# A dynamic 3x3 convolution on 16 images: a larger descriptor scratch for accumulating DMAs, packed small columns, and a new hand-written order of work

## The chip, the cores and the metric

The kernel runs on one core of one Trainium2 chip. The time is the device time of one launch in microseconds (us). Of the kernel before there are three timed runs and one profiled execution.

## What is computed

`x` is (16, 256, 56, 56) float32, the weights are (4, 256, 256, 3, 3) float32: four sets, mixed anew for each image.

```python
def _L0_conv_ref(x, weight, att_w, att_b):
    pooled = jnp.mean(x, axis=(2, 3))
    att = jax.nn.sigmoid(pooled @ att_w.T + att_b)
    agg_w = jnp.einsum('nk,kocij->nocij', att, weight)
    ...                      # one 3x3 convolution per image, stride 1, padding 1
...
def _gn(v, G=32, eps=1e-5):  # per image and group of 8 channels
    ...
    return ((g - m) / jnp.sqrt(s + eps)).reshape(v.shape)
...
x = x + _L0_conv_ref(_gn(x), L0_conv_weight, L0_conv_att_w, L0_conv_att_b)
```

## The kernel before

**Tiling.** The 256 channels are two halves (`c` on the input side, `o` on the output side) of 128 partitions. An image is two chunks of 28 rows. A chunk is convolved along its rows with a transform of six points (`NC` = 6, tables `ORDER`, `POINT`): six transformed inputs `Vs` and six transformed weights `Us`, each split in a high and a low float16 part. For each chunk, point and output half, TensorE runs one `group(e, k, o)` of 18 matmuls of 392 columns (L390); `k` is 0 to 5 for chunk 0 and 6 to 11 for chunk 1, so one step has 24 groups. Six products of high and low parts (3 products by 2 input halves) by three column shifts make up the 18.

**Steps.** `epoch(e)` on each engine convolves image e-1 (in buffer `b`) and prepares image e (in buffer 1-b). There are 16 of them, 14 in a loop that holds two. To prepare an image, VectorE takes the channel statistics (`stats`, L549, eight calls of two instructions; `channel_stats`, L557 writes `mv`), TensorE averages `mv` over the groups (`group_mean_mm`, L342), VectorE and ScalarE turn that into scale and shift (`group_shift`, `group_variance`, `norm_scale`, `attention`), ScalarE normalizes `X` in place (`norm`, L848), TensorE mixes the four weight sets (`mix`, L365, three units) and ScalarE takes the result to `G` (`take_taps`, L842).

**Transformed operands.** VectorE builds an item in one of four buffers `E` (`v_single`, `v_pair` from `X`; `u_pair` from `G`), ScalarE rounds it to float16 (`v_high` L803, `u_high` L809, L813), and VectorE writes the rest (`v_low` L540, `u_low` L534). Points 0 and 5 of the weights need no item.

**Results.** A finished group lies in one of four PSUM banks. ScalarE (`take_first`, `take_pair`) and VectorE (`take_other` L598, `take_edge` L617, `add_rows` L605) combine the groups, and the output rows overwrite `X[b]`. When all rows of one chunk and half stand there, GpSimd issues a DMA that adds the original `x` from DRAM to them (`add_input`, L974, `accum_op`). When this has landed, SyncE stores the rows (L310), and when the store has landed it loads the same place with the image after the next (L303). SyncE goes through this in order: for each chunk store half 0, store half 1, load half 0, load half 1. `add_input` of chunk 1 waits for `("rows", 9, o)`, `("edge", 10, o)` and `("edge", 11, o)`.

**What sets the order.** All order is written out by hand: the tables `E_ITEMS`, `V_LO`, `U_LO`, `V_HI`, `U_HI`, `ACT_TAKES`, `DVE_TAKES` and the bodies of `epoch` on each engine. Each engine works its list strictly in turn, and waits are on counts computed from the tables. On VectorE the statistics of chunk 1 of the next image stand after `take_other(e, 2, 0)`; they are the first instructions that need the loads of the end of the step before.

Of the kernel before, what the change touches and what calls it, by code (L numbers as in the profile page):

```python
# [10 lines left out]
M = 4  # L11
# [67 lines left out]
    (0, 0, 0), (0, 0, 5), (0, 1, 1), (0, 1, 2), (0, 1, 5), (0, 1, 3), (0, 1, 4), (0, 1, 0),  # L79
# [3 lines left out]
    (0, 0, 0), (0, 1, 0), (0, 1, 4), (0, 1, 5), (1, 0, 1), (1, 0, 2), (1, 0, 3), (1, 0, 4),  # L83
    (1, 1, 1), (1, 1, 2), (1, 0, 5), (1, 1, 3),
# [3 lines left out]
    (0, 0), (0, 1), (2, 0), (1, 0), (1, 1), (2, 1), (3, 0), (3, 1),  # L88
    (6, 1), (6, 0), (7, 0), (8, 0), (7, 1), (8, 1), (9, 0), (9, 1),
# [33 lines left out]
def conv_kernel(nc, x, w, att_w, att_b, out):  # L123
# [3 lines left out]
    with ExitStack() as ctx:  # L127
# [19 lines left out]
        attb = sb("attb", [P, 1], F32)  # L147
        nattb = sb("nattb", [P, 1], F32)
        wmax = sb("wmax", [P, CT * JT], F32)
        wtop = sb("wtop", [P, 1], F32)  # L150
        wall = sb("wall", [P, 1], F32)
        ws = sb("ws", [P, 4], F32)
        us = sb("us", [P, 8], F32)
        bn = sb("bn", [P, CT, 8, 6], F32)
        seen = sb("seen", [P, 1], F32)
        mv = sb("mv", [P, CT, 2], F32)
        nmean = sb("nmean", [P, CT], F32)
        rstd = sb("rstd", [P, CT], F32)
        shift = sb("shift", [P, CT], F32)
        off = sb("off", [P, CT], F32)  # L160
        sq = sb("sq", [P, CT], F32)
        spread = sb("spread", [P, CT], F32)
        var = sb("var", [P, CT], F32)
        std0 = sb("std0", [P, CT], F32)
        rs0 = sb("rs0", [P, CT], F32)
        quo = sb("quo", [P, CT], F32)
        std = sb("std", [P, CT], F32)
        rs1 = sb("rs1", [P, CT], F32)
        pooled = sb("pooled", [P, CT], F32)
        ex = sb("ex", [P, 1], F32)  # L170
        ex1 = sb("ex1", [P, 1], F32)
        att = sb("att", [P, 1], F32)
# [9 lines left out]
                   + [X[1][:, i, 1:HP - 1, :].rearrange("p r w -> p (r w)")[:, 0:WG] for i in range(2)])  # L182
# [45 lines left out]
        def rows(b, chunk, i):  # L228
            r = CR * chunk + i
            return [X[b][:, c, r:r + M * (TR - 1) + 1:M, :] for c in range(CT)]  # L230

        def out_rows(b, chunk, o, r):
            q = CR * chunk + 1 + r
            return X[b][:, o, q:q + M * (TR - 1) + 1:M, :]

        def held(b, chunk, c):
            return X[b][:, c, 1 + CR * chunk:1 + CR * (chunk + 1), :].rearrange("p r w -> p (r w)")
# [101 lines left out]
        def _(pe):  # L339
# [56 lines left out]
            def epoch(e, more):  # L396
# [23 lines left out]
                group(e, 7, 1)  # L420
                if more:
                    mix(e, 1)
                group(e, 8, 0)
# [34 lines left out]
        def _(dve):  # L458
# [84 lines left out]
            def stats(e, b, chunk, c, part):  # L543
# [3 lines left out]
                for q in (2 * part, 2 * part + 1):  # L547
                    r = 1 + CR * chunk + TR * q
                    ins = dve.bn_stats(bn[:, c, 4 * chunk + q, :],  # L549
                                       X[b][:, c, r:r + TR, :].rearrange("p r w -> p (r w)"))  # L550
# [70 lines left out]
            def epoch(e, b, more):  # L621
                steps[0] = 0
                v_single(e, b, ("V", 0, 0, 0))
                v_low(e, (0, 0, 4))
                if more:
                    stats(e, 1 - b, 0, 0, 0)
                u_low(e, (0, 0, 0))
                if more:
                    stats(e, 1 - b, 0, 0, 1)
                v_single(e, b, ("V", 0, 0, 5))  # L630
                v_low(e, (0, 0, 0))
                u_low(e, (0, 1, 0))
                if more:
                    stats(e, 1 - b, 0, 1, 1)
                u_low(e, (0, 1, 4))
                v_pair(e, b, ("V", 0, 1, 1))
                take_other(e, 2, 0)
                if more:
                    stats(e, 1 - b, 1, 0, 0)
                    stats(e, 1 - b, 1, 1, 0)  # L640
                    stats(e, 1 - b, 1, 0, 1)
                    stats(e, 1 - b, 0, 1, 0)
                    stats(e, 1 - b, 1, 1, 1)
                take_other(e, 3, 0)
                if more:
                    channel_stats(e)
# [378 lines left out]
```

## Time and profile before

| | |
|---|---|
| median of 3 runs | 1504.98 us (1502.47 to 1506.42) |
| profiled execution | 1503.41 us, of which the span of the trace is 1501.8 us |
| TensorE busy | 89% of the span |
| VectorE busy | 86% |
| ScalarE busy | 45% |
| GpSimd busy | 4% |
| mean granted TensorE clock | 0.959 of full speed |

In the traces PE is TensorE (PEld its weight loads), DVE is VectorE, ACT is ScalarE, POOL is GpSimd, SP is SyncE. A name such as "X<-x_dram" is output and input of an instruction. The number in brackets behind a row of the timeline is the idle time of the engine before it and what ended it; "issue" there means that the engine waited for nothing that the profile shows.

### The profile page before, as it was taken

The page shows a single profiled execution, that of the slowest core. Times are in us where ns is not written, and L with a number is a line of the kernel's source. Part 1 is how long each engine was busy: PE and PEld are TensorE (multiplying, and loading weights), DVE is VectorE, ACT ScalarE, POOL GpSimd, SP SyncE. Part 2 cuts the span into 40 slices and gives each one's busy share as a digit, 9 for nine tenths or more (in the row PEclk, how much of TensorE's full clock was granted, in tenths as well). Part 3 has the DMA queues.
Part 4 walks back from the last instruction along what each step waited for, and adds up shares of the span by engine and source line. Part 5 has one row for each costly group of instructions (what it writes and reads, how often), then busy time and mean ns, then how long its engine had stood idle before and what let it go on. Part 6 is the DMA issues. An engine that isn't in the chain of part 4 may idle for free. (4 is left out here: it accounts for less than half of the span.)

```text
span 1501.8 us, 24616 instructions
## 1 busy us (share of the span) xinstructions
PE 1330.2 (89%) x8808; PEld 743.0 (49%) x8808; DVE 1296.6 (86%) x2211; ACT 669.7 (45%) x922; POOL 59.1 (4%) x77
## 2 busy tenths in 40 slices
PE   0479989899898989989898998989899898998995
PEld 0145545455454545545454554555455454554553
DVE  7999979798997979889798997979899797989961
ACT  2645445363443536344263534426354452634430
POOL 0000000000000000000000000000000000000000
PEclk9989999999999999999999999999999999999998
DMA  8202514445152443515344351544525144451425
GB/s 341 85 2 50 144 65 130 130 121 138 30 149 82 130 129 87 156 36 138 103 129 131 65 140 55 143 116 129 129 50 145 67 129 129 112 146 36 100 61 150
DMA packets 29349, 165.50 MB, mean 110 GB/s; under 512 B 3360, under 2 KB 3616, under 8 KB 28192
## 3 DMA queue, kind: packets, MB, share of 16 engines
q0 software_dynamic: 9216, 51.38, 20.3%
q1 hardware_dynamic: 20000, 112.34, 20.2%
q8 instruction: 84, 1.38, 0.4%
q14 instruction: 49, 0.40, 0.1%
HBM read 112.33 MB, written 51.38 MB: 109 GB/s over the span
## 5 line engine op out<-in xcount | busy, mean ns | idle before, releaser
L390 PE MATMUL pM<-Vs,Us 128*128 128x392 f16 x6912 | 1212.0, 337 | 21.6 <-DVE Us L534 12.8
L390 PEld LDWEIGHTS pM<-Vs,Us 128*128 128x128 f16 x6912 | 678.4, 99 | 543.1 <-issue 60.7
L803 ACT CAST Vs<-E 128x784 f16<-128x784 f32 x192 | 161.8, 843 | 214.7 <-DVE E L509 146.5
L549 DVE BATCH_NORM_STATS2 bn<-X 128x6 f32<-128x392 f32 x256 | 127.2, 555 | 90.2 <-DMA X<-x_dram 90.2
L540 DVE TENSOR_TENSOR Vs<-E,Vs 128x784 f16<-128x784 f32 x192 | 186.4, 971 | 19.3 <-ACT Vs L803 19.3
L483 DVE SCALAR_TENSOR_TENSOR T<-X 128x392 f32<-128x392 f32 x384 | 193.8, 560 | 2.4 <-issue 1.6
L831 ACT ACTIVATE X<-pM,us 128x392 f32<-128x392 f32 x128 | 75.2, 587 | 211.6 <-PE pM L390 211.6
L365 PE MATMUL pG<-W,D 128*32 128x512 f16 x1728 | 103.8, 385 | 30.9 <-DVE W L762 30.9
L813 ACT CAST Us<-E 128x768 f16<-128x768 f32 x128 | 104.5, 828 | 51.1 <-PE pM L390 35.3
L509 DVE SCALAR_TENSOR_TENSOR E<-T 128x784 f32<-128x784 f32 x128 | 119.1, 972 | 3.5
L534 DVE SCALAR_TENSOR_TENSOR Us<-E,Us 128x768 f16<-128x768 f32 x128 | 120.1, 949 | 0.2
L524 DVE SCALAR_TENSOR_TENSOR E<-G,T 128x768 f32<-128x768 f32 x128 | 117.0, 955 | 3.4
L974 POOL DMA_DIRECT2D X<-x_dram x64 | 56.5, 883 | 1393.2 <-DVE X L605 775.3
L848 ACT ACTIVATE X<-X,shift,rstd 128x1568 f32<-128x1568 f32 x64 | 106.4, 1689 | 0.0
L842 ACT ACTIVATE G<-pG 128x512 f32<-128x512 f32 x144 | 80.4, 594 | 25.5 <-PE pG L365 25.2
L342 PE MATMUL pS<-mv,avg 128*128 128x2 f32 x32 | 9.1, 353 | 93.2 <-DVE mv L557 78.3
L365 PEld LDWEIGHTS pG<-W,D 128*32 128x32 f16 x1728 | 42.2, 97 | 84.1 <-DVE W L762 31.4
L852 ACT ACTIVATE std<-var 128x2 f32<-128x2 f32 x16 | 3.3, 203 | 177.2 <-DVE var L569 177.2
L483 DVE SCALAR_TENSOR_TENSOR E<-X,T 128x392 f32<-128x392 f32 x128 | 66.8, 564 | 5.4
L518 DVE SCALAR_TENSOR_TENSOR T<-G 128x768 f32<-128x768 f32 x64 | 60.8, 951 | 0.2
L534 DVE SCALAR_TENSOR_TENSOR Us<-G,Us 128x768 f16<-128x768 f32 x64 | 60.6, 949 | 0.0
L809 ACT ACTIVATE Us<-G 128x768 f16<-128x768 f32 x64 | 53.6, 837 | 14.0 <-PE pM L390 14.0
(65 smaller groups left out, 518.0 us busy)
## 6 DMA issues: line engine op xcount, KB each, us to landing
X<-x_dram SPq DMA_DIRECT2D x64, 784.0 KB, 5.5
X<-x_dram POOLq DMA_DIRECT2D x64, 784.0 KB, 7.8
out_dram<-X SPq DMA_DIRECT2D x64, 784.0 KB, 3.4
W<-w_dram SPq DMA_DIRECT2D x6, 1152.0 KB, 18.2
X<-w_dram SPq DMA_DIRECT2D x2, 1152.0 KB, 26.1
attw<-attw_dram SPq DMA_DIRECT2D x1, 128.0 KB, 8.5
attb<-attb_dram SPq DMA_DIRECT2D x1, 0.5 KB, 10.1
```

What stands on the lines that cost most here:

```text
L365: mm = pe.matmul(dst, D[:, a, :], mix_part(W16[:, :, j, b * WG:(b + 1) * WG], m), start=(a == 0 and b == 0), stop=(a == 1), tile_position= ...
L390: mm = pe.matmul(tile_rows(bank(k, o)), Us[:, j, a, c, o, kx, :], v_in(j, b, c, kx), start=(at < 2 and n == 0), stop=(n == 3 * KS * CT - 1 ...
L483: ins = dve.scalar_tensor_tensor(out=dst[c], in0=a[c], scalar=scale, in1=d[c], op0=ALU.mult, op1=ALU.add)
L509: dve.scalar_tensor_tensor(out=dst, in0=T2[:, :], scalar=POINT[j + m], in1=T1[:, :], op0=ALU.mult, op1=ALU.add).then_inc(e_ready, 1)
L524: dve.scalar_tensor_tensor(out=dst, in0=G[:, c, :, 1, :], scalar=scale, in1=halves(t), op0=ALU.mult, op1=last).then_inc(e_ready, 1)
L534: dve.scalar_tensor_tensor(out=u_flat(j, 1, c), in0=src, scalar=scale, in1=u_flat(j, 0, c), op0=ALU.mult, op1=ALU.subtract).then_inc(u_lo, 1)
L540: dve.tensor_tensor(v_out(v[2], 1), e_planes(("V", *v)), v_out(v[2], 0), ALU.subtract).then_inc(v_lo, 1)
L549: ins = dve.bn_stats(bn[:, c, 4 * chunk + q, :], X[b][:, c, r:r + TR, :].rearrange("p r w -> p (r w)"))
L803: act.copy(v_out(j, 0), e_planes(("V", *v))).then_inc(v_hi, 1)
L813: act.copy(u_flat(j, 0, c), halves(e_buf(("U", *u)))).then_inc(u_hi, 1)
L842: act.mul(mix_part(G[:, :, :, :, :].rearrange("p c o k n -> p c (o k n)"), m), src, MIX_SCALE).then_inc(taps_taken, 1)
L848: act.activation(y, y, ACT.Identity, bias=shift[:, c:c + 1], scale=rstd[:, c:c + 1]).then_inc(normed, 1)
```

## The change

Five things are changed.

1. `dynamic_dma_scratch_size` is 1024 bytes for 512. It is the memory in which GpSimd writes the descriptors of its DMAs.
2. `X` is one tensor: neighbouring halves share one row of zeros, and one strided memset replaces four.
3. Nineteen small tensors are columns of one tensor `small`.
4. On TensorE, `mix(e, 1)` stands between the two halves of k = 7 (it stood behind both), and `mix(e, 2)` behind `group(e, 10, 0)` (it stood behind k = 8).
5. The tables and the lists of VectorE and ScalarE are written in another order. The set of instructions of a step is the same. One item, `("V", 1, 0, 0)`, is now built at the end of a step for the next one, and ScalarE rounds seven weight items at the beginning of the next step that it rounded at the end of the step.

```diff
 DVE_TAKES = [
-    ("other", 2, 0), ("other", 3, 0), ("other", 2, 1), ("other", 3, 1), ("edge", 4, 0),
-    ("edge", 4, 1), ("edge", 5, 0), ("rows", 3, 1), ("edge", 5, 1), ("rows", 3, 0),
-    ("other", 8, 0), ("other", 8, 1), ("other", 9, 0), ("other", 9, 1), ("rows", 9, 0),
-    ("edge", 10, 0), ("edge", 10, 1), ("rows", 9, 1), ("edge", 11, 0), ("edge", 11, 1),
+    ("other", 2, 0), ("other", 2, 1), ("other", 3, 0), ("other", 3, 1), ("edge", 4, 0),
+    ("edge", 4, 1), ("edge", 5, 0), ("rows", 3, 1), ("rows", 3, 0), ("edge", 5, 1),
+    ("other", 8, 0), ("other", 8, 1), ("other", 9, 0), ("other", 9, 1), ("edge", 10, 0),
+    ("rows", 9, 1), ("edge", 10, 1), ("edge", 11, 0), ("edge", 11, 1), ("rows", 9, 0),
 ]
...
-        X = [sb(f"X{b}", [P, CT, HP, W], F32) for b in range(2)]
+        Xs = sb("X", [P, 2 * CT * (HP - 1) + 1, W], F32)
...
-        us = sb("us", [P, 8], F32)
+        small = sb("small", [P, 72], F32)
...
+        us = small[:, 16:24]
...
                 group(e, 7, 0)
+                if more:
+                    mix(e, 1)
                 group(e, 7, 1)
-                if more:
-                    mix(e, 1)
                 group(e, 8, 0)
                 group(e, 8, 1)
-                if more:
-                    mix(e, 2)
                 group(e, 9, 0)
                 group(e, 9, 1)
                 group(e, 10, 0)
+                if more:
+                    mix(e, 2)
                 group(e, 10, 1)
...
-            for b in range(2):
-                dve.memset(X[b][:, :, 0:1, :], 0.0)
-                dve.memset(X[b][:, :, HP - 1:HP, :], 0.0)
+            dve.memset(Xs[:, 0:2 * CT * (HP - 1) + 1:HP - 1, :], 0.0)
...
-    nc = bacc.Bacc("TRN2", target_bir_lowering=False, num_devices=1, dynamic_dma_scratch_size=512)
+    nc = bacc.Bacc("TRN2", target_bir_lowering=False, num_devices=1, dynamic_dma_scratch_size=1024)
```

**VectorE from the last edges of a step on.** First before, the end of the second step in the loop (L605 is `add_rows`, L617 with TA is `take_edge` of k = 11, half 0 and then half 1, L540 is `v_low`, L534 is `u_low`):

```order
L605 SCALAR_TENSOR_TENSOR X<-TB,X 128x7x56 [waits dve_took]
L605 SCALAR_TENSOR_TENSOR X<-TA,X 128x7x56
L612 REGISTER_ALU
L616 REGISTER_ALU [waits dve_took]
L617 SCALAR_TENSOR_TENSOR X<-pM,us,TA 128x7x56 [waits group_done]
L539 REGISTER_ALU
L540 TENSOR_TENSOR Vs<-E,Vs 128x2x7x56 [waits v_hi]
L616 REGISTER_ALU [waits dve_took]
L617 SCALAR_TENSOR_TENSOR X<-pM,us,TA 128x7x56 [waits group_done]
L534 SCALAR_TENSOR_TENSOR Us<-E,Us 128x768 [waits u_hi]
```

and of the changed kernel, from `take_edge` of k = 11, half 1 (L619) to `add_rows` of k = 9, half 0 (L607); L520 and L526 are `u_pair`, L536 is `u_low`:

```order
L619 SCALAR_TENSOR_TENSOR X<-pM,small,TA 128x7x56 [waits group_done]
L481 REGISTER_ALU [waits taps_taken]
L520 SCALAR_TENSOR_TENSOR T<-G 128x768 [waits e_ready]
L466 REGISTER_ALU
L526 SCALAR_TENSOR_TENSOR E<-G,T 128x768 [waits u_lo,dve_step]
L526 SCALAR_TENSOR_TENSOR E<-G,T 128x768 [waits u_lo]
L531 REGISTER_ALU
L536 SCALAR_TENSOR_TENSOR Us<-E,Us 128x768 [waits u_hi]
L531 REGISTER_ALU
L536 SCALAR_TENSOR_TENSOR Us<-E,Us 128x768 [waits u_hi]
L607 SCALAR_TENSOR_TENSOR X<-TB,X 128x7x56 [waits dve_took]
L607 SCALAR_TENSOR_TENSOR X<-TA,X 128x7x56
```

`add_rows(e, b, 9, 0)` stood ahead of all four last edges; it now stands behind the last of them, with one `u_pair` and two `u_low` between.

**VectorE at the statistics that need the last loads.** Before (L598 is `take_other`, L549 `stats`; x_in10 and x_in11 count the loads of chunk 1, halves 0 and 1):

```order
L598 SCALAR_TENSOR_TENSOR TA<-pM,us,TA 128x392 [waits act_took]
L549 BN_STATS bn<-X 128x6 [waits x_in10,mean_ready]
L549 BN_STATS bn<-X 128x6
L549 BN_STATS bn<-X 128x6 [waits x_in11,mean_ready]
...
L549 BN_STATS bn<-X 128x6 [waits x_in01,mean_ready]
...
L598 SCALAR_TENSOR_TENSOR TB<-pM,us,TB 128x392 [waits act_took]
...
L555 COPY seen<-bn 128x1 [waits pieces_ready]
L557 BN_AGGR mv<-bn 128x2 x2
```

and of the changed kernel (L551 `stats`, L600 `take_other`, L536 `u_low` of point 0, L559 the end of `channel_stats`):

```order
L551 BN_STATS bn<-X 128x6 [waits x_in11,mean_ready]
L551 BN_STATS bn<-X 128x6
L599 REGISTER_ALU
L600 SCALAR_TENSOR_TENSOR TA<-pM,small,TA 128x392 [waits act_took]
...
L531 REGISTER_ALU
L536 SCALAR_TENSOR_TENSOR Us<-G,Us 128x768 [waits u_hi]
L551 BN_STATS bn<-X 128x6 [waits x_in10,mean_ready]
...
L600 SCALAR_TENSOR_TENSOR TA<-pM,small,TA 128x392 [waits act_took]
...
L559 BN_AGGR mv<-bn 128x2 x2
```

The statistics of half 1, whose load is the last one, are now the first that need chunk 1, and they stand ahead of the `take_other(e, 2, 0)` that group (4, 0) waits for and of the `u_low(e, (0, 0, 0))` that it needs as weights.

## Rows read from the trace of the kernel before

**Rows 1.** Waits over the whole run: who waited for whom, total us, times, longest.
```profile
POOL X L974 <- issue: 195.6, 31, 6.7
DVE bn L549 <- DMA X<-x_dram: 90.2, 30, 6.2
PE pS L342 <- DVE mv L557: 78.3, 14, 6.9
```

**Rows 2.** Timeline of TensorE, one step: start us, us, instructions [idle before].
```profile
599.78 12.64 PE L390 MATMUL pM<-Vs,Us 128*128 128x392 f16 x74
613.45 27.50 PE L390 MATMUL pM<-Vs,Us 128*128 128x392 f16 x162 [1.03 <-issue]
645.73 0.58 PE L342 MATMUL pS<-mv,avg 128*128 128x2 f32 x2 [4.79 <-DVE mv L557]
646.21 5.35 PE L390 MATMUL pM<-Vs,Us 128*128 128x392 f16 x18
...
664.13 2.12 PE L365 MATMUL pG<-W,D 128*32 128x512 f16 x36
```

**Rows 3.** Timeline of GpSimd over the loop: starts of the accumulating DMAs.
```profile
172.35 0.87 POOL L974 DMA_DIRECT2D X<-x_dram  x1 [26.25 <-DVE X L617]
...
1326.77 0.89 POOL L974 DMA_DIRECT2D X<-x_dram  x1 [26.63 <-DVE X L617]
```

**Rows 4.** The same view, the pair of chunk 1 at the step of rows 2.
```profile
616.13 0.89 POOL L974 DMA_DIRECT2D X<-x_dram  x1 [26.50 <-DVE X L617]
623.57 0.88 POOL L974 DMA_DIRECT2D X<-x_dram  x1 [6.56 <-issue]
```

**Rows 5.** Timeline of SyncE's DMA queue, the stores and loads behind that pair.
```profile
623.41 9.24 SPq L310 DMA_DIRECT2D out_dram<-X  x2
632.84 3.83 SPq L303 DMA_DIRECT2D X<-x_dram  x2
```

**Rows 6.** Timeline of VectorE, same step: last edges and the two waits for loads.
```profile
615.30 0.97 DVE L540 TENSOR_TENSOR Vs<-E,Vs 128x784 f16<-128x784 f32 x1
616.18 0.62 DVE L617 SCALAR_TENSOR_TENSOR X<-pM,us,TA 128x392 f32<-128x392 f32 x1
616.72 0.95 DVE L534 SCALAR_TENSOR_TENSOR Us<-E,Us 128x768 f16<-128x768 f32 x1
...
638.30 1.04 DVE L549 BATCH_NORM_STATS2 bn<-X 128x6 f32<-128x392 f32 x2 [4.54 <-DMA X<-x_dram]
640.74 3.84 DVE L549 BATCH_NORM_STATS2 bn<-X 128x6 f32<-128x392 f32 x8 [1.41 <-DMA X<-x_dram]
```

**Rows 7.** Windows: busy us and instructions of each engine, granted clock, DMA share, GB/s.
```profile
617.50:623.00 5.50, 5.50 (x34) 3.22 (x33) 5.15 (x10) 2.73 (x4) 0.00 (x0) 1.00 0.87 150
624.00:626.00 2.00, 2.00 (x14) 1.14 (x13) 1.88 (x5) 0.00 (x0) 0.45 (x1) 1.00 0.90 364
626.00:631.50 5.50, 5.50 (x34) 3.16 (x33) 5.46 (x10) 2.28 (x4) 0.00 (x0) 1.00 0.93 160
632.00:642.00 10.00, 8.94 (x54) 4.98 (x51) 4.05 (x8) 5.13 (x7) 0.00 (x0) 1.00 0.69 241
```

**Rows 8.** Timeline of VectorE: starts from which the lengths of its items are read.
```profile
683.69 0.95 DVE L518 SCALAR_TENSOR_TENSOR T<-G 128x768 f32<-128x768 f32 x1
...
686.42 0.62 DVE L598 SCALAR_TENSOR_TENSOR TA<-pM,us,TA 128x392 f32<-128x392 f32 x1
...
695.72 1.99 DVE L483 SCALAR_TENSOR_TENSOR T<-X 128x392 f32<-128x392 f32 x4
...
699.52 0.62 DVE L617 SCALAR_TENSOR_TENSOR X<-pM,us,TB 128x392 f32<-128x392 f32 x1
```

**Rows 9.** Windows around the wait of TensorE; the columns are those of rows 7.
```profile
643.90:650.70 6.80, 4.97 (x16) 2.57 (x17) 5.96 (x15) 0.00 (x0) 0.00 (x0) 0.50 0.01 2
```

**Rows 10.** Timelines of TensorE where the loop begins, and of GpSimd at the end.
```profile
84.97 5.41 PE L390 MATMUL pM<-Vs,Us 128*128 128x392 f16 x16 [12.83 <-DVE Us L534]
...
1482.57 0.88 POOL L974 DMA_DIRECT2D X<-x_dram  x1 [17.08 <-DVE X L617]
```

More of the change, by code:

```diff
@@ L622, in epoch @@
                 steps[0] = 0
-                v_single(e, b, ("V", 0, 0, 0))
-                v_low(e, (0, 0, 4))
+                v_single(e, b, ("V", 0, 0, 5))
+                u_low(e, (0, 1, 4))
                 if more:
                     stats(e, 1 - b, 0, 0, 0)
-                u_low(e, (0, 0, 0))
-                if more:
-                    stats(e, 1 - b, 0, 0, 1)
-                v_single(e, b, ("V", 0, 0, 5))
+                    stats(e, 1 - b, 0, 1, 1)
+                v_pair(e, b, ("V", 0, 1, 1))
                 v_low(e, (0, 0, 0))
@@ L676, in epoch @@
                 v_low(e, (0, 1, 4))
+                v_low(e, (0, 1, 0))
                 if more:
@@ L679, in epoch @@
                     v_low(e, (1, 0, 1))
-                    u_low(e, (1, 0, 1))
                 take_other(e, 8, 0)
                 if more:
+                    u_low(e, (1, 0, 1))
+                    u_low(e, (1, 0, 2))
                     v_low(e, (1, 0, 2))
-                    u_low(e, (1, 0, 2))
+                    v_pair(e, 1 - b, ("V", 1, 0, 3))
                     u_pair(e, ("U", 1, 0, 3))
+                    v_low(e, (1, 0, 4))
                 take_other(e, 8, 1)
                 if more:
-                    u_low(e, (1, 0, 3))
+                    v_low(e, (1, 0, 3))
+                take_other(e, 9, 0)
+                take_other(e, 9, 1)
+                take_edge(e, b, 10, 0)
+                add_rows(e, b, 9, 1)
+                if more:
                     u_pair(e, ("U", 1, 1, 1))
-                take_other(e, 9, 0)
-                if more:
                     u_low(e, (1, 0, 4))
-                take_other(e, 9, 1)
-                add_rows(e, b, 9, 0)
-                take_edge(e, b, 10, 0)
-                if more:
-                    u_low(e, (1, 1, 2))
-                    u_low(e, (1, 1, 1))
-                    v_pair(e, 1 - b, ("V", 1, 0, 3))
                 take_edge(e, b, 10, 1)
                 if more:
-                    u_pair(e, ("U", 1, 1, 3))
-                add_rows(e, b, 9, 1)
+                    u_low(e, (1, 1, 1))
                 take_edge(e, b, 11, 0)
                 if more:
-                    v_low(e, (1, 0, 3))
+                    u_low(e, (1, 0, 3))
                 take_edge(e, b, 11, 1)
                 if more:
+                    u_pair(e, ("U", 1, 1, 3))
+                    u_low(e, (1, 1, 2))
                     u_low(e, (1, 1, 3))
+                add_rows(e, b, 9, 0)
+                if more:
+                    v_single(e, 1 - b, ("V", 1, 0, 0))
                 assert steps[0] == STEPS or not more, steps
@@ L769, in _ @@
             u_low(0, (1, 0, 1))
+            u_low(0, (1, 0, 2))
             v_low(0, (1, 0, 2))
-            u_low(0, (1, 0, 2))
+            v_pair(0, 0, ("V", 1, 0, 3))
             u_pair(0, ("U", 1, 0, 3))
-            u_low(0, (1, 0, 3))
+            v_low(0, (1, 0, 4))
+            v_low(0, (1, 0, 3))
             u_pair(0, ("U", 1, 1, 1))
             u_low(0, (1, 0, 4))
+            u_low(0, (1, 1, 1))
+            u_low(0, (1, 0, 3))
+            u_pair(0, ("U", 1, 1, 3))
             u_low(0, (1, 1, 2))
-            u_low(0, (1, 1, 1))
-            v_pair(0, 0, ("V", 1, 0, 3))
-            u_pair(0, ("U", 1, 1, 3))
-            v_low(0, (1, 0, 3))
             u_low(0, (1, 1, 3))
+            v_single(0, 0, ("V", 1, 0, 0))
             first[0] = steps[0]
@@ L881, in epoch @@
                 if more:
-                    norm(e, 1 - b, 1, 0)
-                v_high(e, (0, 1, 4))
-                if more:
-                    norm(e, 1 - b, 0, 1)
+                    norm(e, 1 - b, 1, 1)
                     norm(e, 1 - b, 0, 0)
@@ L888, in epoch @@
                 if more:
-                    norm(e, 1 - b, 1, 1)
+                    norm(e, 1 - b, 1, 0)
                     take_taps(e, 0)
-                take_first(e, 6, 1)
-                if more:
                     take_taps(e, 1)
                     take_taps(e, 2)
+                    norm(e, 1 - b, 0, 1)
                 take_first(e, 6, 0)
@@ L897, in epoch @@
                     take_taps(e, 3)
+                v_high(e, (0, 1, 4))
+                take_first(e, 7, 1)
                 take_first(e, 7, 0)
```

178 lines of the change are left out of this document (86 added, 92 removed), and 8 rows, old and new, of the table E_ITEMS.

## The prediction

> **What bounds the kernel now.** I read the waits first, then the timelines of one step, then the windows. The steps are regular: from the first accumulating DMA of chunk 1 at 172.35 to the same at 1326.77 are 13 steps, 88.80 us each [rows 3]. TensorE has no room apart from one hole. In the step shown it ends the step before at 599.78 + 12.64 = 612.42, runs nine groups (162 matmuls in 27.50 us, 3.06 us a group), then stands for 4.79 us until `mv` is there [rows 2]. The engine's granted clock is at half, its lower level of 1.2 GHz, from about 643.9 to 650.7 [rows 9]: the next group takes 5.35 us instead of 3.1, so the hole costs about 2.1 us more. Without both the step would be some 81 us. `mv` is late because VectorE waits for loads: 90.2 us in all, two waits a step, here 4.54 and 1.41 us [rows 1, 6]. VectorE itself has little room too. Its waits in this step are 5.95 for loads and some 3.2 others, so it works 79.6 us of 88.8. So the last loads set the step, through VectorE, and both engines are close behind.
>
> The loads hang on a chain that I call C, from the first accumulating DMA of chunk 1 to the statistics that need the last load: 616.13 to 640.74, 24.6 us [rows 4, 6]. In it GpSimd starts the second accumulation only at 623.57, after 6.56 us "for nothing that the profile shows" [rows 4]; there are 31 such waits, 195.6 us [rows 1]. That wait ends just after the first store starts at 623.41 [rows 5], which needs the first accumulation landed: the second waits until the first is done. The larger scratch is meant for this.
>
> **Part 1, the scratch.** If it works, the second issue moves from 623.57 to about 617.0, 6.5 us earlier. The gain in C is less, since the DMA engines are not idle meanwhile. The first accumulation holds all 16 for 5.5 x 0.87 = 4.8 us, the store of half 0 for 2.0 x 0.90 = 1.8, the second accumulation for 5.5 x 0.93 = 5.1, the rest (one store, two loads) for 10 x 0.69 = 6.9 [rows 7]. That is 18.6 us of work, with 1.4 before the first packet (616.13 to 617.5): C can hardly be under 20.0, or 19.6 if the start of the second, for which the engines need some time, hides behind the first transfer. In the worst case it has no such cover and shares the engines with the first store: the gain is then only the gap between the transfers and what the engines leave idle, about 2 us, and C = 22.6. I take 21.0, near the sum of work plus one latency of 1.0 us that stays between landing and the next issue (the first transfer leaves the engines at about 622.5, the store starts at 623.41 [rows 5, 7]). So the gain is 3.6 us of the 6.5.
>
> The Trainium skill says the same of any two transfers at once ("DMA: Bandwidth & Descriptors", section "Rules for kernel authors"): two transfers to disjoint parts serialize, because both spread over the same 16 engines. Taken strictly it speaks against the purpose of this change; the 0.87 and 0.93 of rows 7 agree with it. By the rule alone C would be at its upper end.
>
> **Part 2, VectorE's order ahead of C.** This is a loss. Lengths, from start to start [rows 6, 8]: `u_pair` 686.42 - 683.69 = 2.73, `v_pair` 699.52 - 695.72 = 3.80, `v_low` 0.88, `u_low` 0.87 (0.01 less, as it is 2% shorter), edge 616.72 - 616.18 = 0.54. One `stats` is a quarter of 3.84 less its overlap, 0.94 [rows 6]. The others go by kind: `add_rows` is two instructions of 392 columns, 0.95; `take_other` reads 392 columns of PSUM as the edge does, 0.53; `v_single` is four instructions of 392 columns and one wait between, 1.99 and 0.16 [rows 8], 2.15. Call P the end of the last group of a step. Before, the edge of half 0 stood at 615.30 less 0.54, and C began at P + 3.7 (612.42 to 616.13). Now the first add_input also waits for `add_rows(9, 0)`, which stands last: edge 0.1 + 0.54, `u_pair` 2.73, two `u_low` 1.74, two rows 1.03, GpSimd 0.2. C begins at P + 6.3, if VectorE has caught up with TensorE. That is 2.6 us later.
>
> **Part 3, VectorE's order behind C.** Between the start of C and the first statistics that need the last load VectorE has, less the 0.2: two `v_single` 4.3, two `u_low` 1.74, four `stats` 3.8, `v_pair` 3.8, `v_low` 0.88, together 14.5 us. C is 21.0, so VectorE waits about 6.5 us (before: 5.95). Worse, the half asked for first is now the later one, and `take_other(2, 0)` and `u_low(0, 0, 0)`, for which group (4, 0) waits, stand behind that wait. Call t the landing of the last load. `stats` 0.94, `take_other` 0.53, `stats` 0.94, `u_low` 0.87 and the latency give group (4, 0) at t + 3.4. Then come 3.1 for the group and 0.5 for the mean; `mv` is ready at t + 6.3 and no longer in the way. TensorE is at group (4, 1) at t + 7.0 plus the slow clock. Before, it was there at 646.21 - 640.74 = t + 5.5 [rows 2, 6]. The rest of the step, from group (4, 1) at 646.21 to the next P at 612.42 + 88.8 = 701.2, is 55.0 us, with about 2 us of slow clock in it, which now falls mostly on group (4, 0). So the next P is at t + 62.0 on TensorE. On VectorE: 79.6 of work less 20.6 between the last edge and t is 59.0, and I find waits of 0.3 and 1.3 for the two group averages, 1.0 for the last `norm`, which now stands behind three `take_taps`, and 0.5 for an item rounded late: t + 62.1. Both ends meet; I take 62.0.
>
> **The step.** 6.3 + 21.0 + 62.0 = 89.3 us, 0.5 more than 88.8. From P to P there are 14 such intervals: 7.0 us.
>
> **Part 4, the rest.** The mixes are moved on TensorE alone: 2.06 us each, 36 matmuls as before [rows 2], with nothing new late behind them: `take_first` and `take_taps` come 1 us or more ahead of need, `u_pair(1, 1, 1)`, which now needs the third unit, stands 2 us behind it. Cover gone, each us costs 14. The loop starts at 84.97 on TensorE, released by a `u_low` of VectorE [rows 10]. Ahead of that one, VectorE now has a `v_pair` and two `v_low` more and two `u_low` fewer: 3.8 + 1.76 - 1.74 = 3.8, of which I count 3.5, as the first groups run on a slow clock (16 matmuls in 5.41). At the end, C's head is cut by 3.6 but begins about 4 us later relative to the last group, since `add_input` waits for rows behind the last edge and the first accumulation no longer runs beside the last group (1482.57 [rows 10]): +0.5. The shared zero row takes three short memsets away, at a place where VectorE then waits for the loads of x: nothing. The packed columns change no instruction: nothing, between -0.1 and +0.1.
>
> **Sum.** 1501.8 + 7.0 + 3.5 + 0.5 = 1512.8 of span, and 1.6 outside it as before (1503.41 less 1501.8): **1514.4 us**. The profiled execution is 1.6 below the median of the runs, so this may be read as 1516 against 1504.98; I stay with the trace.
>
> **Rivals.**
> *The transfers truly overlap* (this one ends faster). If the second accumulation ends about a store's time or less after the first, C falls below 20.2, where the longer start is paid back. At C = 19.6: step 87.9, 1514.4 - 14 x 1.4 = 1494.8 us. If it landed 1 us behind the first, C = 17.1 and 1460 us. For it: in the engines' work the accumulation moves only 150 to 160 GB/s, the store 364 [rows 7], so the engines spend their time on something that two transfers might share. Against it: they are busy 0.87 and 0.93. Chance 0.22.
> *The steps lock in at no change.* C between 20.2 and 20.7, or a shorter stay at the low clock: the low stretch is 6.8 us wide and TensorE stands in part of it [rows 9]. If TensorE stands 6 us instead of 4.8, less of it hits work; up to 1 us a step. 1501 to 1509 us. Chance 0.17.
> *The scratch does not do it* (the wait comes from something else). C stays 24.6, while the order is made for less: step 92.9, 14 x 3.6 = 50 more, 1565 us. For it: the row only says "issue". Against it: the wait ends with the landing each time. Chance 0.05.
> *The two accumulations stay strictly one behind the other and behind the first store*, as the rule above has it. C is 22.6, the step 90.9: 1514.4 + 14 x 1.6 = 1536.8 us. For it: 0.87 and 0.93 busy. Against it: 1.4 us of start-up that can hide. Chance 0.06.
> *VectorE falls behind in the second half.* It has some 0.7 us to spare where group (10, 1) waits for `take_other(8, 1)`, and 1.1 us where group (1, 0) waits for `u_low(1, 1, 3)` behind the last edge. Waits of ScalarE that I place wrongly come out there. 1 us a step more is 1528, 1.5 is 1535. Chance 0.14.
> The forecast itself, 1509 to 1524: 0.36.
>
> **How the numbers follow.** A measurement of this kernel can tell about 0.3%, 4.5 us, from no change: 1500.5 to 1509.5. Faster is the first rival, 0.22; same is the second, 0.17; slower are the forecast and the last three, 0.36 + 0.05 + 0.06 + 0.14 = 0.61. The range takes in C from 19.4 to 22.8 and leaves out 0.09 below (C under 19.4) and 0.09 above (no effect of the scratch, and a late VectorE beyond 1.8 us a step): 1492 to 1540.
>
> **What the profile would show.** GpSimd's "issue" waits of 6.3 us gone, the second accumulation 0.9 to 1.0 us behind the first (part 1). The first of chunk 1 at P + 6.3 (part 2). C from 19.6 to 22.6, and about 14 waits for loads of 6 to 7 us at the statistics of half 1, with almost none behind (part 3). TensorE's hole ahead of group (4, 0), about 6 us, put down to VectorE's `Us` or `take_other`, and none at the mean. The loop starting near 88.5. I am wrong if C comes out under 20, if TensorE stands anywhere in the second half of a step, or if the second issue still waits.

## The result and the profile after

The changed kernel takes 1509.41 us (median of 19 runs, 1505.4 to 1516.5), the kernel before in the same sessions 1505.19 us (19 runs). The ratio is 1.0032, with a 95% interval from 1.0019 to 1.0044: slower by 0.3%, 4 to 5 us. The span of the profiled execution is 1510.1 us, 8.3 more than before. The forecast was 1514.4 us.

A small difference, but not a small change. Waits over the whole run after, as in [rows 1]:

```profile
DVE bn L551 <- DMA X<-x_dram: 91.8, 16, 8.9
DVE T L485 <- issue: 13.0, 6, 2.4
PE pM L392 <- DVE Us L536: 113.2, 19, 15.5
```

The 195.6 us in which GpSimd waited for nothing that the profile shows are gone. The wait for the loads has stayed as it was, 91.8 us for 90.2, now nearly all in one wait a step. TensorE's hole has moved from the mean of the groups to group (4, 0), where it waits for `u_low(0, 0, 0)` (L536), and has grown from 78.3 us to 95 in the 14 steps (the 113.2 also hold the 15.5 ahead of the first step and some short waits).

Timeline of GpSimd after: the first pair of chunk 1, one in the middle, and the last but one (rows 3 and 4 show the same of before).

```profile
178.84 1.77 POOL L969 DMA_DIRECT2D X<-x_dram  x2 [36.20 <-DVE X L607]
...
892.62 1.77 POOL L969 DMA_DIRECT2D X<-x_dram  x2 [36.65 <-DVE X L607]
...
1426.77 1.76 POOL L969 DMA_DIRECT2D X<-x_dram  x2 [36.71 <-DVE X L607]
```

Both DMAs of a pair start in one piece of 1.77 us. From 178.84 to 1426.77 are 14 steps of 89.14 us in the mean. Before, the same 14 took 1414.97 - 172.35, 88.76 us each. The 14 steps after are not alike: eleven take 88.4 to 89.1 us, 88.76 in the mean and so as much as before, and three take 90.3 to 90.7. In two of these three the granted clock of TensorE is low for 10.2 us, from 643.6 and from 1357.0, where it is low for 6.8 in all others; in the third the chain C takes 22.6 us. The step shown below is one of the eleven (88.68 us).

Timeline of TensorE in the step of 892.62 (as [rows 2]):

```profile
883.78 26.14 PE L392 MATMUL pM<-Vs,Us 128*128 128x392 f16 x154
916.90 4.72 PE L392 MATMUL pM<-Vs,Us 128*128 128x392 f16 x18 [6.98 <-DVE Us L536]
921.46 0.28 PE L344 MATMUL pS<-mv,avg 128*128 128x2 f32 x2
921.60 3.20 PE L392 MATMUL pM<-Vs,Us 128*128 128x392 f16 x18
```

and of VectorE there (as [rows 6]):

```profile
885.90 0.62 DVE L619 SCALAR_TENSOR_TENSOR X<-pM,small,TA 128x392 f32<-128x392 f32 x1
886.44 0.95 DVE L520 SCALAR_TENSOR_TENSOR T<-G 128x768 f32<-128x768 f32 x1
...
891.38 0.56 DVE L607 SCALAR_TENSOR_TENSOR X<-TA,X 128x392 f32<-128x392 f32 x1
...
913.40 1.04 DVE L551 BATCH_NORM_STATS2 bn<-X 128x6 f32<-128x392 f32 x2 [7.11 <-DMA X<-x_dram]
914.36 0.61 DVE L600 SCALAR_TENSOR_TENSOR TA<-pM,small,TA 128x392 f32<-128x392 f32 x1
914.88 1.03 DVE L551 BATCH_NORM_STATS2 bn<-X 128x6 f32<-128x392 f32 x2
915.83 0.94 DVE L536 SCALAR_TENSOR_TENSOR Us<-G,Us 128x768 f16<-128x768 f32 x1
```

The last edge stands at 885.90, the rows that `add_input` waits for at 891.38, the chain C begins at 892.62 and ends at 913.40: 20.8 us. VectorE stands 7.11 us for the last load. Only behind it come `take_other` and the `u_low` at 915.83 that lets TensorE go on at 916.90. Its group then takes 4.72 us, since the clock is low; this is the window as in [rows 9]:

```profile
914.90:921.80 6.90, 4.90 (x22) 2.57 (x23) 6.90 (x15) 0.00 (x0) 0.00 (x0) 0.63 0.00 0
```

SyncE's queue behind the pair, as [rows 5], and the DMA engines in windows that begin about with the pair's packets, as [rows 7]; the second window overlaps the first a little:

```profile
899.77 4.12 SPq L312 DMA_DIRECT2D out_dram<-X  x2
905.47 3.77 SPq L305 DMA_DIRECT2D X<-x_dram  x2
```

```profile
894.00:903.00 9.00, 9.00 (x55) 5.18 (x53) 8.93 (x16) 1.81 (x3) 0.39 (x1) 1.00 1.01 201
902.30:908.00 5.70, 5.70 (x36) 3.32 (x34) 4.00 (x7) 4.04 (x7) 0.00 (x0) 1.00 0.98 348
908.00:914.20 6.20, 1.92 (x12) 0.88 (x9) 0.80 (x2) 2.84 (x4) 0.00 (x0) 0.92 0.59 202
```

The two stores start 7.15 us and 10.9 us behind the first accumulation (before: 7.3 and 16.2). Up to 908 the engines are busy 1.01 and 0.98 of the time, for 0.87 to 0.93 before: no gap is left between the accumulations and the first store. Behind that, to the landing of the last load, they are busy 0.59.

### The profile page after: what moved, and what is told of

Its sections match the earlier page's. It is cut to its first block, busy times and chain, and to the rows that moved or that the text cites. A ratio compares the mean times of both kernels' runs of the same rounds, so it can differ in the third digit from the quotient of the medians.

```text
span 1510.1 us, 24711 instructions
## 1 busy us (share of the span) xinstructions
PE 1322.8 (88%) x8808; PEld 738.8 (49%) x8808; DVE 1297.8 (86%) x2208; ACT 674.2 (45%) x922; POOL 59.6 (4%) x77
## 3 DMA queue, kind: packets, MB, share of 16 engines
q0 software_dynamic: 9216, 51.38, 18.2%
## 4 chain that ended last, share of the span: by engine, by line
PE 42%; DVE 24%; DMA 18%; issue 12%; ACT 1%; DVEq 1%; POOL 0%; POOLq 0%; SPq 0%; ACTq 0%
PE pM L392 38%; DMA X<-x_dram 14%; PE pG L367 4%; DVE Us L536 4%; DMA out_dram<-X 4%; DVE E L526 3%; DVE T L520 3%; DVE T L485 3%; DVE Vs L542 2%; DVE X L607 2%; DVE X L619 2%; DVE E L511 1%; DVE bn L551 1%; DVE TA L600 1%; DVE W L762 1%
## 5 line engine op out<-in xcount | busy, mean ns | idle before, releaser
L392 PE MATMUL pM<-Vs,Us 128*128 128x392 f16 x6912 | 1210.2, 337 | 115.6 <-DVE Us L536 113.2
L551 DVE BATCH_NORM_STATS2 bn<-X 128x6 f32<-128x392 f32 x256 | 127.0, 554 | 91.8 <-DMA X<-x_dram 91.8
L833 ACT ACTIVATE X<-pM,small 128x392 f32<-128x392 f32 x128 | 75.2, 588 | 172.6 <-PE pM L392 155.4
L536 DVE SCALAR_TENSOR_TENSOR Us<-E,Us 128x768 f16<-128x768 f32 x128 | 120.1, 950 | 2.9 <-ACT Us L815 1.5
L526 DVE SCALAR_TENSOR_TENSOR E<-G,T 128x768 f32<-128x768 f32 x128 | 116.9, 954 | 2.2
L850 ACT ACTIVATE X<-X,small 128x1568 f32<-128x1568 f32 x64 | 106.4, 1688 | 0.0
L854 ACT ACTIVATE small<-small 128x2 f32<-128x2 f32 x16 | 3.3, 206 | 186.8 <-DVE small L571 186.8
L520 DVE SCALAR_TENSOR_TENSOR T<-G 128x768 f32<-128x768 f32 x64 | 61.0, 952 | 7.6 <-ACT G L844 6.8
L825 ACT ACTIVATE TA<-pM,small 128x392 f32<-128x392 f32 x64 | 37.6, 588 | 52.7 <-PE pM L392 49.4
L536 DVE SCALAR_TENSOR_TENSOR Us<-G,Us 128x768 f16<-128x768 f32 x64 | 58.5, 933 | 2.2 <-ACT Us L811 2.2
```

The lines of the kernel that those rows point to most:

```text
L392: mm = pe.matmul(tile_rows(bank(k, o)), Us[:, j, a, c, o, kx, :], v_in(j, b, c, kx), start=(at < 2 and n == 0), stop=(n == 3 * KS * CT - 1 ...
L520: step(e, dve.scalar_tensor_tensor(out=halves(t), in0=G[:, c, :, 2, :], scalar=p * p, in1=G[:, c, :, 0, :], op0=ALU.mult, op1=ALU.add))
L526: dve.scalar_tensor_tensor(out=dst, in0=G[:, c, :, 1, :], scalar=scale, in1=halves(t), op0=ALU.mult, op1=last).then_inc(e_ready, 1)
L536: dve.scalar_tensor_tensor(out=u_flat(j, 1, c), in0=src, scalar=scale, in1=u_flat(j, 0, c), op0=ALU.mult, op1=ALU.subtract).then_inc(u_lo, 1)
L551: ins = dve.bn_stats(bn[:, c, 4 * chunk + q, :], X[b][c][:, r:r + TR, :].rearrange("p r w -> p (r w)"))
L850: act.activation(y, y, ACT.Identity, bias=shift[:, c:c + 1], scale=rstd[:, c:c + 1]).then_inc(normed, 1)
```

## The experiments

All times are medians; ratios are to the kernel before on the same chip. "The changed kernel" stands for 1509.4 us. The kernel before took 1505.1, 1505.8 and 1507.4 us on the three chips used, so a difference between two edited kernels can come out some 2 to 4 us otherwise by the medians than by the ratios.

**The scratch alone, in the order of before.** The kernel before with `dynamic_dma_scratch_size=1024`, `Xs` and `small`, none of the tables or lists changed.

```diff
-    nc = bacc.Bacc("TRN2", target_bir_lowering=False, num_devices=1, dynamic_dma_scratch_size=512)
+    nc = bacc.Bacc("TRN2", target_bir_lowering=False, num_devices=1, dynamic_dma_scratch_size=1024)
```

> The kernel before in its own order of work, with the scratch of 1024 bytes (and, to make room for it, the shared zero rows and the packed columns). Chain theory (the step is set by the chain C from the first accumulating DMA of chunk 1 to the statistics of the last load, and VectorE's work behind it): C falls from 24.6 to 21.0 us while it begins where it did, 3.7 us after the last group P. VectorE's waits for loads fall from 6.0 to about 2.4 us a step; the step is 21.0 + 64.2 = 85.2 us, 14 x 3.6 = 50 us less: 1452 us. Order theory (the new order is needed for the gain): it stays at 1500 to 1505 us. Clock theory (TensorE's low clock gives back what a shorter wait wins, steps stay at 88.7 us): 1500 to 1505 us.

Measured: 1443.83 us, ratio 0.959 (0.956 to 0.963). Its wait for the loads:

```profile
DVE bn L551 <- DMA X<-x_dram: 39.4, 29, 2.9
```

and the timeline of GpSimd, the pair of chunk 1 in one step:

```profile
682.61 0.88 POOL L974 DMA_DIRECT2D X<-x_dram  x1 [32.80 <-DVE X L619]
684.12 0.88 POOL L974 DMA_DIRECT2D X<-x_dram  x1 [0.63 <-issue]
```

So the scratch brings 61 us, and the new order costs 66. The waits for loads fall from 90.2 to 39.4 us as expected. C is 21.1 us in the mean of the 14 steps. The time is 8 us under the forecast of 1452, since 63.4 us are left behind C for the 64.2 that were expected. TensorE's hole is shorter, and the low clock with it: 3.4 us long in ten steps and absent in four, for 6.8 us in each before (mean granted clock 0.978 for 0.959). The order theory and the clock theory, both at 1500 or more, fall.

**The packing alone.** As before, with 512 bytes.

```diff
-        X = [sb(f"X{b}", [P, CT, HP, W], F32) for b in range(2)]
+        Xs = sb("X", [P, 2 * CT * (HP - 1) + 1, W], F32)
...
-        attb = sb("attb", [P, 1], F32)
+        small = sb("small", [P, 72], F32)
```

> The kernel before with the shared zero rows and the packed columns alone: scratch of 512 bytes, the order of before. By the prediction's part 4 this changes nothing: 1503 to 1507 us. The rival reading of before_scratch (that part of its gain comes from the packing and not from the scratch) wants under 1500 us.

Measured: 1509.14 us beside 1505.8, ratio 1.0012 (0.9992 to 1.0032): no difference that can be told. The interval would allow one as large as that of the whole change (1.0032); in the trace the 14 steps take 88.67 us each, no more than before, so there is none in the steps.

**The changed kernel with 512 bytes.**

```diff
-    nc = bacc.Bacc("TRN2", target_bir_lowering=False, num_devices=1, dynamic_dma_scratch_size=1024)
+    nc = bacc.Bacc("TRN2", target_bir_lowering=False, num_devices=1, dynamic_dma_scratch_size=512)
```

> The changed kernel with the scratch of 512 bytes again. Chain theory: GpSimd's waits of some 6.3 us for nothing that the profile shows return, C is 24.6 us for 21.0, the step 92.8 us, 14 x 3.6 = 50 us more than the changed kernel: 1560 us. Theory that two accumulations at once gain nothing since both use the same 16 DMA engines: 1510 us. Clock theory: 1510 to 1525 us.

Measured: 1575.22 us, ratio 1.045 (1.043 to 1.048). Its waits:

```profile
POOL X L969 <- issue: 209.9, 32, 7.7
DVE bn L551 <- DMA X<-x_dram: 151.0, 15, 12.4
```

The waits of GpSimd are back, 6.6 us each, and VectorE's wait for the loads is 10.6 us a step for 6.3. That is 66 us for the scratch in this order, 15 more than forecast. C is 25.1 us in the mean for the 24.6 of the forecast, and with a hole of 11 us instead of 7 TensorE spends longer at the low clock: 10.2 or 13.7 us a step for 6.8 (0.935 in the mean).

**`add_rows` of k = 9, half 0 ahead of the last edges again.**

```diff
-    ("other", 8, 0), ("other", 8, 1), ("other", 9, 0), ("other", 9, 1), ("edge", 10, 0),
-    ("rows", 9, 1), ("edge", 10, 1), ("edge", 11, 0), ("edge", 11, 1), ("rows", 9, 0),
+    ("other", 8, 0), ("other", 8, 1), ("other", 9, 0), ("other", 9, 1), ("rows", 9, 0), ("edge", 10, 0),
+    ("rows", 9, 1), ("edge", 10, 1), ("edge", 11, 0), ("edge", 11, 1),
...
+                add_rows(e, b, 9, 0)
                 take_edge(e, b, 10, 0)
...
                     u_low(e, (1, 1, 3))
-                add_rows(e, b, 9, 0)
```

> The changed kernel with add_rows of k = 9, half 0 ahead of the last four edges, where it stood before the change (and so in the table of takes). Chain theory: C begins at about P + 0.2 us for P + 7.0, its length stays 21 us, so the last load lands 6.8 us earlier; VectorE waits for it about 1 to 2 us for 6.1, group (4, 0) on TensorE comes almost without a hole, the step is bound by VectorE's 79.6 us of work and its other waits, 83 to 84.5 us: 1430 to 1450 us. Theory that the place of add_rows does not matter (C's end is set elsewhere): 1505 to 1512 us.

Measured: 1437.22 us, ratio 0.955 (0.953 to 0.957), in the range of the chain theory. Two instructions, 1 us together, moved in VectorE's list are worth 72 us. The steps are no longer alike, 81 to 83 and 85 to 88 us in turn. The timeline of VectorE where the loop begins anew shows why:

```profile
429.38 1.04 DVE L485 SCALAR_TENSOR_TENSOR T<-X 128x392 f32<-128x392 f32 x2
430.45 1.04 DVE L485 SCALAR_TENSOR_TENSOR E<-X,T 128x392 f32<-128x392 f32 x2
436.10 1.04 DVE L485 SCALAR_TENSOR_TENSOR T<-X 128x392 f32<-128x392 f32 x2 [4.61 <-issue]
```

VectorE stands 4.61 us ahead of the first instruction behind the loop's edge, six times in the run, at every second step; before it was 1.6 us in all six.

**The half that lands last asked for last.**

```diff
                     stats(e, 1 - b, 0, 0, 1)
-                    stats(e, 1 - b, 1, 1, 1)
                 take_other(e, 2, 0)
-                if more:
-                    stats(e, 1 - b, 1, 1, 0)
                 u_low(e, (0, 0, 0))
                 if more:
                     stats(e, 1 - b, 1, 0, 0)
                     stats(e, 1 - b, 1, 0, 1)
+                    stats(e, 1 - b, 1, 1, 1)
+                    stats(e, 1 - b, 1, 1, 0)
```

> The changed kernel with take_other(2, 0) and u_low(0, 0, 0) ahead of the statistics of chunk 1, and of these half 0 ahead of half 1. C is untouched. Chain theory: group (4, 0) starts without a wait, the hole of 7 us ahead of it is gone and one of some 3.5 us comes ahead of the mean of the groups; after the last load VectorE has 3.3 us less to do, so the step is 3.3 to 3.6 us shorter, 85.5 us: 1459 us. Theory that only the start and length of C count: 1505 to 1510 us.

Measured: 1464.72 us, ratio 0.974 (0.972 to 0.976). Its waits:

```profile
PE pS L344 <- DVE mv L559: 44.8, 14, 5.2
DVE bn L551 <- DMA X<-x_dram: 41.6, 26, 3.4
PE pM L392 <- DVE Us L536: 17.6, 5, 15.5
```

The hole is ahead of the mean again, 3.2 us a step for 7, and the one ahead of group (4, 0) is gone. The pairs of chunk 1 start at 179.19 and 1376.28 in this kernel's timeline, 14 steps of 85.5 us, which is the forecast. "Only start and length of C count" falls: who stands behind the wait counts too.

**Filling the hole.** 24 matmuls on old operands ahead of group (4, 0) in the changed kernel; then 36.

```diff
+                if more:
+                    keep_clock(24)
                 group(e, 4, 0)
```

> The changed kernel with 24 matmuls on old operands, 384 columns each (about 4 us), ahead of group (4, 0), so in the hole of about 7 us in which TensorE stands; nothing waits for them. Clock theory (the low clock behind the hole is what sets the step): group (4, 0) takes 3.1 us again for 4.8 to 6.0, the step is 1.7 to 2.9 us shorter: 1470 to 1487 us. Chain theory (VectorE sets the step; TensorE's slow group costs it only its wait of 0.9 us for the variance and the long low stretches of two steps): 1492 to 1503 us. If the clock does not care: 1509 us.

Measured: 1517.36 us, ratio 1.007 (1.005 to 1.010): a miss for every theory. The timeline of TensorE in one step:

```profile
736.77 2.11 PE L440 MATMUL pS<-W 128*128 128x384 f16 x12
742.74 4.83 PE L392 MATMUL pM<-Vs,Us 128*128 128x392 f16 x18 [3.86 <-DVE Us L538]
```

3.86 us of the hole are left, and group (4, 0) still takes 4.83 us. The clock is low for only 3.4 us in most steps, but from 742.7 here, so wholly on the group. The edit didn't keep the clock up where TensorE works, so it doesn't show what the low clock costs. Its own cost is in the trace: the first pair of chunk 1 starts 3.7 us later than in the changed kernel (182.53 for 178.84), as the fillers of the first step stand ahead of it, and the 14 steps take 89.39 us each for 89.14, which adds 3.5.

```diff
+                if more:
+                    keep_clock(36)
                 group(e, 4, 0)
```

> As filler with 36 matmuls (5.8 us) in the hole, so that about 1.2 us of it is left. With 24, group (4, 0) still took 4.8 us in most steps (a low stretch of 3.4 us that fell wholly on it), and in the one step where it took 3.2 us the step was 87.9 us instead of 89.3. If the clock can be kept up by this, group (4, 0) takes 3.1 to 3.2 us in most steps and these are 87.9 us: about 14 x 1.3 = 18 us less than the changed kernel, and some 6 more in the first step, where the fillers run slowly: 1495 to 1500 us. If VectorE alone sets the step: 1510 to 1516 us.

Measured: 1502.4 us, ratio 0.996 (0.994 to 0.998), so 7 us under the changed kernel by the medians and 11 by the ratios. The timeline and the window:

```profile
641.19 6.01 PE L440 MATMUL pS<-W 128*128 128x384 f16 x36
648.14 3.21 PE L392 MATMUL pM<-Vs,Us 128*128 128x392 f16 x18 [0.94 <-DVE Us L538]
```

```profile
640.00:665.00 25.00, 23.71 (x147) 14.11 (x145) 20.01 (x45) 5.77 (x8) 0.00 (x0) 1.00 0.10 35
```

Now the granted clock is full, the group takes 3.21 us. The 14 steps take 87.94 us each for 89.14, 1.2 us less; 6.7 us of the gain are lost again ahead of the first pair of chunk 1 (185.5 for 178.84), as the first fillers run at the low clock. So the low clock behind the hole costs 1.2 us a step. That is part of the 4.7 us a step by which this order is slower than that of before with the same scratch, and not most of it.

**Both corrections of the order together.** The edits of the two experiments on `add_rows` and on the statistics in one kernel; in `epoch` on VectorE:

```diff
+                add_rows(e, b, 9, 0)
                 take_edge(e, b, 10, 0)
...
-                add_rows(e, b, 9, 0)
...
-                    stats(e, 1 - b, 1, 1, 1)
...
-                    stats(e, 1 - b, 1, 1, 0)
...
                     stats(e, 1 - b, 1, 0, 1)
+                    stats(e, 1 - b, 1, 1, 1)
+                    stats(e, 1 - b, 1, 1, 0)
```

> rows_early and stats_swap together. In rows_early the steps go 87 and 82 us in turn; in the longer one VectorE stands 4.6 to 4.9 us for nothing that the profile shows where its loop begins anew, 5 us behind the start of the accumulations. Chain theory with that wait as the new bound: the last load is no longer waited for, but the steps behind the loop's edge keep their 4.8 us on VectorE: 1420 to 1430 us. If the two edits add up (71 and 45 us less than the changed kernel): 1393 us. If rows_early had taken all there is: 1437 us.

Measured: 1424.33 us, ratio 0.945 (0.943 to 0.948). They don't add up, as the wait at the loop's edge is now the bound. The waits:

```profile
DVE T L485 <- issue: 29.1, 6, 5.0
...
DVE bn L551 <- DMA X<-x_dram: 3.5, 2, 3.1
```

**The same with the loop written out.**

```diff
-            with dve.Fori(0, (N - 2) // 2) as i:
+            for i in range((N - 2) // 2):
                 epoch(i * 2 + 1, 0, True)
                 epoch(i * 2 + 2, 1, True)
```

and so on the other four engines.

> As both, with the 14 steps of the loop written out on all engines, so that no engine jumps back. If the wait of 4.8 us on VectorE is the fetch of instructions at the jump, behind the DMAs in flight, it is gone, and every step is near TensorE's 81 to 82.5 us: 1402 to 1415 us. If it is something else that falls on these steps, the time is that of both. If code that is written out has to be fetched everywhere and waits more often: slower than both.

Measured: 1394.95 us, ratio 0.926 (0.924 to 0.928), 111 us less than the kernel before and under the forecast by 7. One step in the windows:

```profile
577.80:658.80 81.00, 80.50 (x549) 45.29 (x548) 78.23 (x137) 40.91 (x58) 3.52 (x4) 1.00 0.43 120
```

TensorE is busy 80.5 of 81.0 us at full clock, and VectorE's only wait for a load is the 3.1 us of the first image. This is the best version found, and its steps are at TensorE's own length.

**The changed kernel with the loop written out.** The same edit in the changed kernel, all else as it is.

```diff
-            with dve.Fori(0, (N - 2) // 2) as i:
+            for i in range((N - 2) // 2):
```

> The changed kernel with the 14 steps of its loop written out. VectorE stands 2.1 us at each of 6 edges of the loop for nothing that the profile shows (13.0 us in all), but in those steps it then waits less for the loads, since the chain C runs on meanwhile. If C sets the step, the time stays within 3 us of the changed kernel: 1506 to 1512 us. If the edges cost in full: 1496 us.

Measured: 1507.95 us, ratio 1.0004 (0.9985 to 1.0023), in the range that the chain wants. The edit removes VectorE's 13.0 us of waits at the edges, and its wait for the loads grows from 91.8 to 98.0 us:

```profile
DVE bn L551 <- DMA X<-x_dram: 98.0, 16, 8.0
```

Of the 13.0 us removed 1.5 come out in the time by the medians, and 4 by the ratios (1.0004 for 1.0032): a wait taken away ahead of a longer one is worth little.

**The best version with 512 bytes.**

```diff
-    nc = bacc.Bacc("TRN2", target_bir_lowering=False, num_devices=1, dynamic_dma_scratch_size=1024)
+    nc = bacc.Bacc("TRN2", target_bir_lowering=False, num_devices=1, dynamic_dma_scratch_size=512)
```

> both_unrolled with the scratch of 512 bytes. C is 24.6 us again, and VectorE comes to the statistics that need the last load 23.6 us behind its start: it waits 1 us, TensorE 0.5 to 1 us ahead of the mean of the groups. If the scratch is worth only what the order leaves uncovered: 1402 to 1416 us. If it is worth its 3.6 to 4.7 us a step in any order: 1445 to 1460 us.

Measured: 1410.88 us, ratio 0.936 (0.934 to 0.938). The waits:

```profile
POOL X L968 <- issue: 207.2, 32, 7.3
...
DVE bn L551 <- DMA X<-x_dram: 16.9, 24, 3.3
...
PE pS L344 <- DVE mv L559: 11.3, 13, 1.8
```

GpSimd waits its 207.2 us as ever, and the kernel loses 16. The scratch is worth 66 us in the changed order, 61 in that of before, and 16 here, where VectorE's wait for the loads grows by only 13.8 us (3.1 to 16.9): what the order leaves uncovered.

**The order of before, with the scratch and without the loop.** The same edit in the kernel of the first experiment.

```diff
-            with dve.Fori(0, (N - 2) // 2) as i:
+            for i in range((N - 2) // 2):
```

> before_scratch with the loop written out: the order of before, two accumulations in flight, no jumps. VectorE's wait at the edge is 0.3 us there, TensorE's 1.2 us stands ahead of group (0, 0), and in both cases the chain through the loads has the last word: 1436 to 1442 us, 2 to 8 less than before_scratch. If the order of before is as good as both_unrolled's once nothing jumps: 1395 to 1405 us.

Measured: 1429.84 us, ratio 0.949 (0.946 to 0.952). That is 14 us under its looped form (16 by the ratios), where 2 to 8 were expected, and 35 us over the best version. Its waits at VectorE's edges were only 1.8 us in all and TensorE's 4.8; where the rest of the gain comes from isn't shown. So the order of before is not as good as the mended new one, but far better than the new one as it came.

## Why the prediction was right, point by point

**What bounds the kernel** held. Each edit that moves the start of C, its length or what stands behind it moved the time as this reading wants. As long as C was the bound, taking VectorE's waits at the loop's edge away gave next to nothing; once it was not (`both`), the same edit gave 29 us.

**Part 1** held best. C was put at 21.0 us, with a gain of 3.6: in the step shown it is 913.40 - 892.62 = 20.8, and in the mean of the 14 steps 21.0 (20.2 to 22.6). The second store starts 10.9 us behind the first accumulation for 16.2 before, and the gap in the DMA engines' work between the two accumulations is gone. The first rival, that the two truly overlap, and the strict one, at C = 22.6, both fall. A little of the first is true all the same: by the pages' shares the 64 accumulations take 4.8 us of the engines each before (20.3% of 1501.8 us) and 4.3 after (18.2% of 1510.1), and the kernels with either scratch in the other orders agree (4.7 to 4.8 and 4.3).

The rule of the Trainium skill ("DMA: Bandwidth & Descriptors", section "Rules for kernel authors"), that two transfers to disjoint partition halves serialize since they share the same 16 engines, agrees with a share of 1.01 in the window of the two accumulations, though each of them here fills all 128 partitions. It doesn't say what the chain gains: the start-up of the second transfer and the idle gap.

**Part 2**, the later start, was right in kind and too small: 6.7 us from the last edge at 885.90 to the start of C, for 6.2 in the sum. The term at fault is GpSimd's latency, 0.2 us; it starts 0.8 us behind the end of the rows (891.38 + 0.48 to 892.62). The rows before had shown it: 615.30, where the instruction behind the edge of half 0 begins, to 616.13 [rows 4, 6] is 0.8 us too. That is 7 us over 14 steps too little.

**Part 3** was right in its mechanism: a wait at the statistics of half 1 and none behind, a hole ahead of group (4, 0), no hole at the mean. The wait is some 7 us in one step and 5 in the next, since VectorE also stands 2.2 us at the loop's edge in every second step. The prediction did not have that wait; it costs little, because the last load lands no later for it. Group (4, 0) comes 3.5 us behind the last load (3.4 in the sum). The length behind the landing was too high: 89.14 less 6.8 ahead of C and 21.0 for C leaves 61.3 us for 62.0. VectorE's work was right. A step less its waits is 79.1 to 79.9 us in all 14, for the 79.6 of the sum. The waits were too many: behind the landing in the step shown they are 0.89 for a group average, 0.82 for `norm` and 0.45 for `take_taps`, 2.2 in all, where 0.3, 1.3, 1.0 and 0.5 had been put. The two errors, 0.5 too little in part 2 and 0.7 too much here, nearly cancel: the step was forecast as 89.3 and is 89.1 in the mean.

**Part 4.** The start of the loop on TensorE was put 3.5 us later. It stands at 89.43 for 84.97, and the later low clock gives 1.4 us of that back until the first step ends:

```profile
89.43 2.79 PE L392 MATMUL pM<-Vs,Us 128*128 128x392 f16 x8 [15.51 <-DVE Us L536]
```

Four traces in the order of before, with and without the packing, start the loop between 84.97 and 87.45, and six in the new order between 89.11 and 90.72, so 3.5 is right as far as it can be read. The packing costs nothing that can be told (1.0012, with 1 in the interval). The 0.5 us at the end is less than can be read.

**The sum**, term by term in the span: 14 steps 5.3 us (7.0 in the forecast), the rest 3.0 (4.0), together 8.3 for 11.0. The forecast of 1514.4 lies 5 us over the median.

**How much of the hit is luck.** By the medians the change is 4.2 us where 9.4 were forecast (1514.4 less 1504.98). The spans look better than that, because the profiled execution after lies 2.3 us above its median and the one before 1.6 below. The 0.5 us more in every step did not come either: eleven steps are as long as before, and the 5.3 us are three long steps, two of them by a longer stretch of low clock. The rival in which the steps lock in at no change (C between 20.2 and 20.7, 1501 to 1509 us, chance 0.17) comes close to these eleven, in which C is 20.8 in the mean, and the median of 1509.4 lies where that rival and the forecast meet. So the chain, its start and its end are shown by the experiments; that their sum came out a little slower, and not level, rests on terms that cancel to within 0.2 us.

**What I had not seen.** The price of the order was put at 2.6 + 1.5 us a step, 57 in all, and it is 66 us, 4.7 a step. I counted these losses in the sum, but did not say that the scratch alone, with nothing else, would be the better kernel by 4%; the same rows would have given it: 21.0 + 64.2 us.

## What to carry to other kernels

When a chain of transfers sets the step, look at three things apart: what the first transfer waits for, how long the chain is, and which instructions stand behind the wait at its end; here two instructions, 1 us together, that stood behind the last edges instead of ahead of them cost as much as the whole gain of the larger scratch. If a change brings a resource and a new order at once, measure the resource alone first. A wait in the list of waits is worth only what no other wait covers: the same 200 us of GpSimd's waits were worth 66, 61 and 16 us.

## What the runs showed of the hardware

- A hole on TensorE costs more than its length. With one of 7 us the granted clock goes to half, and the next group takes 4.7 us instead of 3.2; with 36 matmuls in it the clock stays at full in 13 of 14 steps, and a step is 1.2 us shorter. With 24, which left 3.86 us, it did not stay up.
- The larger scratch lets GpSimd issue its second accumulating DMA 0.9 us behind the first (1.5 in the order of before, where half 1 is finished later); with 512 bytes it waits until the first has landed, 6.3 to 6.6 us in the mean, in the three orders tried.
- Where VectorE's loop begins anew it stands for nothing that the profile shows, and how long differs with the order: 0.3 us in the kernel before and with the scratch alone, 2.2 us in the changed kernel, and 4.6 to 5.0 us with `add_rows` early, where the edge comes 7.2 us behind the start of a pair of accumulations. With the loop written out these waits are gone and the best order is 29 us faster.
- What goes with the end of these waits is in the traces. A DMA packet of 8 KB of the kind "instruction" (queue q14 of the page) starts 2.0 to 2.9 us ahead of the first instruction behind the edge, at all 60 edges of the ten traces with a loop, whether VectorE stood there 0.2 or 5.0 us. Where it stood some 2.2 us, the packet starts within 0.1 us of its stop (once 0.4); with `add_rows` early it starts 2.6 to 2.9 us after the stop. So that VectorE waits there for its next instructions is supported, though no run takes that load apart from the rest. What holds the packet back with `add_rows` early isn't shown: with the scratch alone the edge lies 1.6 us behind the start of a pair of accumulations, in the changed kernel 1.3 us, and the waits are 0.2 and 2.4 us.
